# Score tiles of four heads with 32 queries each instead of two heads with 64, in an attention kernel on one core

## The reference

```python
# x: (4, 1024, 512); 16 query heads, 8 key heads, 128 plain and 64 rotated places a head
xn = layernorm(x)
c_Q = rms_norm(xn @ Wq_down, q_norm_w)                 # 192 wide
q_nop, q_pe = c_Q @ Wq_up, c_Q @ Wq_pe                 # 16 heads x 128, 16 heads x 64
c_KV = rms_norm(xn @ Wkv_down, kv_norm_w)              # 128 wide
k_nop, v = split(c_KV @ Wkv_up)                        # 8 heads x 128 each, used by two query heads
k_pe = rms_norm(xn @ Wk_pe, k_pe_norm_w)               # 64, shared by all heads
q = concat(q_nop, rope(q_pe)); k = concat(k_nop, rope(k_pe))
scores = (q . k) / sqrt(192), masked to k <= q
y = softmax(scores) @ v
out = x + y @ Wo + ternary(xn) @ (ternary(weight) + rram).T
```

## Time and profile before

| | |
|---|---|
| median of 3 runs | 1685.34 us (1685.02 to 1686.73) |
| the profiled execution | 1687.18 us, its span 1685.4 us |
| PE busy | 1647.7 us, 98% of the span |
| DVE busy | 1309.9 us, 78% |
| ACT busy | 1117.6 us, 66% |
| GpSimd busy | 599.7 us, 36% |
| matmuls | 11656 |

### The profile page before, as it was taken

The page is one execution under the profiler, slowest core; times in us unless marked ns, Lnnn a source line. Parts: engine busy times, 40 slices in busy tenths (PEclk is TensorE's granted clock), DMA queues, the critical chain, the costliest instruction groups (busy, mean ns, idle before and its releaser), DMA issues.

```text
span 1685.4 us, 34179 instructions
## 1 busy us (share of the span) xinstructions
PE 1647.7 (98%) x11656; PEld 929.4 (55%) x11656; DVE 1309.9 (78%) x3369; ACT 1117.6 (66%) x2464; POOL 599.7 (36%) x1080
## 2 busy tenths in 40 slices
PE   5989999999999999999999999999999999999999
PEld 5755555555555556555554555555555555655544
DVE  5888878768788788778878787876878878877765
ACT  5877767567676676657667676766767667666663
POOL 2433334333343333433433333433334333343330
PEclk9999999999999999999999999999999999999999
DMA  9346777758768677786759867775876867776776
GB/s 261 88 74 114 128 133 126 131 109 144 136 126 148 115 132 133 147 135 105 141 102 156 144 127 133 129 128 109 147 133 131 147 112 134 136 138 132 132 134 123
DMA packets 780264, 221.25 MB, mean 131 GB/s; under 512 B 766968, under 2 KB 769402, under 8 KB 779770
## 3 DMA queue, kind: packets, MB, share of 16 engines
q1 hardware_dynamic: 769392, 195.41, 66.9%
q10 hardware_dynamic: 9162, 17.37, 3.5%
q0 software_dynamic: 1536, 6.29, 1.1%
HBM read 19.76 MB, written 8.39 MB: 17 GB/s over the span
## 4 chain that ended last, share of the span: by engine, by line
PE 86%; DVE 4%; issue 3%; ACT 2%; POOL 2%; DMA 2%; SPq 0%; DVEq 0%; ACTq 0%; POOLq 0%
PE bank L729 7%; PE bank L731 7%; PE bank L730 7%; PE bank L732 7%; PE bank L827 6%; PE bank L829 6%; PE bank L828 6%; PE bank L774 5%; PE bank L776 5%; PE bank L775 5%; PE bank L742 4%; PE bank L484 2%; PE bank L485 2%; PE bank L785 1%; PE bank L523 1%
## 5 line engine op out<-in xcount | busy, mean ns | idle before, releaser
L1116 ACT ACTIVATE P<-P,nm 128x256 f32<-128x256 f32 (+15 forms) x512 | 381.8, 746 | 409.9 <-DVE nm L1520 409.1
L1520 DVE CUSTOM_DVE_ANT_0 P<-bank,mask,neg 128x256 f32<-128x256 f32 (+15 forms) x512 | 383.1, 783 | 244.6 <-PE bank L742 237.8
L1769 POOL TENSOR_SCALAR sn<-sm 128x1 f32<-128x1 f32 x512 | 207.8, 406 | 888.3 <-ACT P L1116 877.4
L1111 ACT ACTIVATE F<-P,rc 128x256 f16<-128x256 f32 (+15 forms) x512 | 365.2, 741 | 102.3 <-DVE rc L1528 64.1
L1534 DVE SCALAR_TENSOR_TENSOR F<-P,rc,F 128x256 f16<-128x256 f32 (+15 forms) x512 | 402.4, 798 | 2.8 <-ACT F L1111 2.4
L729 PE MATMUL bank<-K,Q 128*128 128x512 f16 (+7 forms) x760 | 241.7, 319 | 0.0
L732 PE MATMUL bank<-K,QP 128*128 128x512 f16 (+7 forms) x760 | 241.7, 319 | 0.0
L730 PE MATMUL bank<-K,Q 128*128 128x512 f16 (+7 forms) x760 | 241.7, 319 | 0.0
L731 PE MATMUL bank<-K,Q 128*128 128x512 f16 (+7 forms) x760 | 241.7, 319 | 0.0
L827 PE MATMUL bank<-WO,YH 128*128 128x512 f16 x512 | 194.3, 379 | 5.0 <-DVE YL L1540 4.7
L828 PE MATMUL bank<-WO,YH 128*128 128x512 f16 x512 | 194.0, 379 | 0.0
(11 more groups left out here) (228 smaller groups left out, 3248.9 us busy)
## 6 DMA issues: line engine op xcount, KB each, us to landing
out<-X ACTq DMA_DIRECT2D x31, 256.0 KB, 2.8
X<-in_x ACTq DMA_DIRECT2D x28, 256.0 KB, 4.1
FT<-F SPq DMA_TRANSPOSE x348, 4.2
wo<-in_Wo POOLq DMA_DIRECT2D x4, 1024.0 KB, 7.1
V<-CC SPq DMA_DIRECT2D x64, 32.0 KB, 2.9
QP<-QS SPq DMA_TRANSPOSE x128, 2.7
X<-in_x SPq DMA_DIRECT2D x4, 256.0 KB, 8.4
kv<-in_Wkv_up POOLq DMA_DIRECT2D x1, 1024.0 KB, 12.3
```

The lines of the kernel that those rows point to most:

```text
L1111: return e.eng.activation(dst, src, ACT.Copy, scale=scale)
L1116: e.eng.activation(m.P[:, u % 4, 0:w], m.P[:, u % 4, 0:w], ACT.Exp, bias=m.nm[:, u % 8:u % 8 + 1], scale=-1.0, accum_out=m.sm[:, u % 8:u % ...
L1520: e.eng.tensor_tensor_reduce(out=m.P[:, u % 4, 0:w], in0=m.pS[u % 2][:, off:off + w], in1=m.mask[:, end - w:end], scale=m.neg[:, :], scala ...
```

## The change

Score tiles now hold four heads with 32 queries each. The rows of x are loaded in plain order. `row_block(u)` is 0, 2, 1, 3 for u%4 = 0, 1, 2, 3, and `columns` takes 96, 64, 32 or 0 keys off for row block 0, 1, 2, 3, in all units.

- `queries_hi`, `queries_lo`, `values_hi` and `values_lo` sort between "by heads" and "by rows" in pieces of 32; the stride of two that `values_hi` and `values_lo` wrote with is gone.
- SP turns `QS` into a new tile `QT`, and DVE copies that in the new order to `QP` (`rotated_rows`, L1351 of the changed kernel). In body n it does so for unit n+3, ahead of the two maxima of half 1. PE waits for that copy (`s.qp`), no longer for the DMA.
- `rotated_hi` and `rotated_lo` are two instructions each, on 64 partitions each.
- Columns between a tile's cut and the end of what is weighed have to be zero: GpSimd's `zero_gap(u)` (a MEMSET into `F`) follows `scale_sum(u)`. It waits until the slot of `F` has been turned (`ft_in`). In ordinary units there is one for u%4 = 0 and 1, in whole ones for 0, 1 and 2; 268 in all.
- GpSimd waits for its own results in a few places (`sm`, `gap`, `pl`).
- `keep_keys` and `KT` are gone: SP turns the keys into `K` directly. The values go to `V` in one DMA instead of two.
- `weigh_pair` waits for all four tiles of the last unit.

```diff
 def columns(u):
-    return blocks_wide(u) - (64 if side(u) == 0 and not whole(u // 4) else 0)
+    return blocks_wide(u) - 96 + 32 * row_block(u)
...
     def pair(n, p):
-        e.wait_ge(s.q_in[n % 2], 16 * (n // 2 + 1))
-        e.wait_ge(s.k_at, n // NG + 1)
+        e.wait_ge(s.qp, n + 1)
+        e.wait_ge(s.k_in, 16 * (n // NG + 1))
...
     def weigh_pair(p):
-        for z in (GROUP_OF[4 * n + p], GROUP_OF[4 * n + p + 2]):
+        for z in range(GROUP_OF[4 * n], GROUP_OF[4 * n + 3] + 1):
             e.wait_ge(s.ft_in[z % FSLOTS], 16 * (z // FSLOTS + 1))
...
     def rotated_hi(self, n):
-        e.eng.activation(rotated_parts(m, n)[0], m.R1.rearrange("p (g h) d -> p g h d", g=2), ACT.Copy).then_inc(s.ph, 1)
+        for a in range(2):
+            op = e.eng.activation(rotated_parts(m, n, a)[0], m.R1[64 * a:64 * a + 64, :, :], ACT.Copy)
+        op.then_inc(s.ph, 1)
...
+    def rotated_rows(self, n):
+        e, m, s = self.e, self.m, self.s
+        e.wait_ge(s.q_in[n % 2], 16 * (n // 2 + 1))
+        if n >= 2:
+            e.wait_ge(s.s, 4 * (n - 1))
+        e.eng.tensor_copy(m.QP[:, n % 2, :, :].rearrange("p r (h k) -> p r h k", k=32),
+                          m.QT[:, n % 2, :, :].rearrange("p h (r k) -> p r h k", k=32)).then_inc(s.qp, 1)
...
+    def zero_gap(u):
+        slot, z, at = parts_place(u)
+        w, lo, end = columns(u), blocks_wide(u), gap_end(u)
+        if end == w:
+            return
+        if z >= FSLOTS:
+            e.wait_ge(s.ft_in[slot], 16 * (z // FSLOTS))
+        both = m.F[:, slot, at:at + 2 * lo].rearrange("p (x c) -> p x c", x=2)
+        e.eng.memset(both[:, :, w:end], 0.0).then_inc(s.gap, 1)
...
     outputs_lo(15)
+    queries.rotated_rows(2)
     for n in range(N):
...
+            if p and n + AHEAD + 1 < N:
+                queries.rotated_rows(n + AHEAD + 1)
             if u < 4 * N:
                 maximum(u)
```

## The result

The changed kernel takes **1699.25 us** (median of 4, 1697.59 to 1699.96) against 1685.5 for the kernel before in the same runs: ratio 1.0076, 95% interval 1.0064 to 1.0088. It is 13.8 us slower by the medians (10.8 to 14.8 by the interval), where 1687.4 was forecast, and lies outside the range, 1678 to 1694. The profiled execution took 1699.09 us with a span of 1697.1.

The account below looks back on a forecast made before the run. TensorE, busy 98% of the span, was taken as the bound, so time is columns plus its waits. Columns −13.9, start +3.9, repeats +9.6 and end +2.5 sum to +2.1 on 1685.34: 1687.4 us, range 1678 to 1694.

Parts of the forecast that it names:

- Columns, −13.9: TensorE's score passes over the whole kernel: fewer columns from the new cuts save 13.9 us.
- the 29 that was charged: Some 60 passes of 32 columns on TensorE: charged 29 ns each instead of 16, taking 0.8 us off the saving.
- The end, +2.5: First `weigh_pair` of the last unit: it now waits for the last tile, costing 2.5 us net.
- the clock decides nothing: Whole kernel: the granted clock stands at its full 2.4 GHz in every slice, so it was given no cost.
- The second `rotated_hi`: ScalarE's chain to `queries_hi`: the added instruction delays it by 0.31 us, between 0 and 0.40.
- The copy: VectorE ahead of half 1's maxima: 0.35 us, free where VectorE idles, counted in full where it is busy.
- The start, +3.9: From `pair(2, 0)` through the first bodies: the late copy and longer chains add 3.9 us of waiting and lost saving.
- The repeats, +9.6: Three repeats where a long tile precedes short ones: longer chains add 3.2 us of waits each, 9.6 in all.
- The 0.06 us that was read as cover near 836: Second part of a repeat: TensorE starts 0.06 us after `values_lo` ends, taken as all the slack there.
- That waits don't add up: Rival for the repeats: one longer wait shrinks the next, so they cost 2.6 us in all; 1680.4 us, chance 0.33.
- The meeting with GpSimd: Rival: the copy runs beside GpSimd's work and takes 0.33 us more in 19 places; 1693 us, chance 0.20.
- GpSimd's stall on the gap: Rival: `zero_gap` waits and holds up `scale_sum`, 0.1 us in each of 116 units' bodies; 1695 us or more, chance 0.05.

Follow-up runs that it names:

- e8_both: Changed kernel without VectorE's copy (TensorE reads QT directly) and with one `rotated_hi` and one `rotated_lo`, some score parts on wrong rows: 1671.80 us.
- b12_end: Kernel before the change, with only `weigh_pair` made to wait for all four tiles of the last unit: 1689.05 us.
- b11_hi2: Kernel before the change, with only `rotated_hi` split into two instructions of 64 partitions: 1712.57 us.
- e3_one: Changed kernel with `rotated_hi` and `rotated_lo` as one 128-partition instruction each, half the rows having high and low parts swapped: 1675.39 us.
- e14_apart: Changed kernel with the first `rotated_hi` left ahead of `queries_hi` and the second moved behind `values_hi`: 1692.58 us.
- e2_late: Changed kernel with the copy of half 1 moved from ahead of the two maxima to behind them: 1693.51 us.
- e13_behind: Changed kernel with both `rotated_hi` behind `queries_hi`, and behind `values_hi` too where that stands next: 1694.91 us.
- e15_behind_late: e13_behind with the copy moved behind the two maxima: 1691.53 us.
- e4_nogap: Changed kernel without the MEMSETs of the gaps from unit 20 on, so stale numbers are weighed there: 1699.44 us.

## Why the prediction was wrong

- **Columns, −13.9: right.** Undisturbed bodies are 0.09 to 0.10 us shorter, and a pass of 32 columns starts 0.03 us before the next, no more than one of 64. The mean over the passes is 26 ns against 29, so the 29 that was charged was near, and the 16 by the formula alone is not what the trace shows:

```profile
775.12 0.18 PE L729 MATMUL bank<-K,Q 128*128 128x32 f16 x1
775.15 0.18 PE L730 MATMUL bank<-K,Q 128*128 128x32 f16 x1
```

  With the copy and both second instructions out (e8_both), the loop is 15.7 us shorter than before, MEMSETs and all: 2 more than its columns, as it waits a little less.
- **The end, +2.5: right**, 2.5 us of waiting at L810 and b12_end. The profiled execution lost 1.5 more there at half the clock, which nobody had priced: the prediction took the page's slices to say that the clock decides nothing.
- **The second `rotated_hi`: this is the step that failed.** It was put at 0.31 us and counted only where TensorE already waited for `queries_lo`, 3 times outside the start. It is 0.54 us, and it opened waits for `queries_lo` in 15 places where none stood, and small delays in 42 bodies (b11_hi2); alone it costs 24.3 to 26.0 us, where all work added outside the end was put at 13.5. VectorE waited for `queries_hi` 60 times before and TensorE felt it in 7 places; the others were taken to have ample slack, and b11_hi2 shows that in 15 more there was less than what one instruction adds. The delay also isn't over when TensorE has been served: `queries_lo` stands ahead of `values_lo`, the next maxima and `scaled_lo` in VectorE's list, and in bodies of short tiles these have no idle time in between. In body 42 of the changed kernel VectorE comes to the first maximum of half 1 8.10 us after the body's start, in e3_one 7.57, before the second instruction of that body is even run. How the rest of its cost comes about is open, as e14_apart shows.
- **The copy: its length was right, its wait was missed.** 0.35 us was taken, 338 ns is the mean and 0.29 the usual value. The prediction never looked when the DMA of QT lands. Before, QP had until TensorE's next pair; now VectorE needs it half a body earlier, and where SyncE has x, keys and values to move first it isn't there, in 29 of 128 cases, all in the fourth unit of a tile (bodies 3, 7, 11 and on). SyncE's timeline ahead of the one in body 43:

```profile
597.92 1.44 SPq L1839 DMA_TRANSPOSE XT<-XS  x1
599.53 1.45 SPq L1859 DMA_TRANSPOSE C<-CC  x1
601.03 1.26 SPq L1861 DMA_TRANSPOSE K<-CC  x1
602.33 0.60 SPq L1863 DMA_DIRECT2D V<-CC  x1
603.10 3.07 SPq L1923 DMA_TRANSPOSE FT<-F  x1
606.29 1.20 SPq L1905 DMA_TRANSPOSE QT<-QS  x1
```

  The maxima stand behind the copy. In the changed kernel's timeline of VectorE:

```profile
608.76 0.29 DVE L1351 COPY QP<-QT 128x512 f16<-128x512 f16 x1 [2.65 <-DMA QT<-QS]
609.10 0.68 DVE L1536 CUSTOM_DVE_ANT_0 P<-bank,mask,neg 128x448 f32<-128x448 f32 x1
```

  The maximum starts at once; before, in the same body, it waited 3.22 us for TensorE. The 2.65 us mostly replace that idle time: moving the copy (e2_late) gave 5.7 us in all, not 61.
- **The start, +3.9: too small.** The copies for units 0 and 1 hold the first score by 1.65 us, and the one for unit 2 `pair(2, 0)` by 1.87:

```profile
77.76 0.19 PE L708 MATMUL bank<-K,Q 128*128 128x32 f16 x1 [1.65 <-DVE QP L1351]
...
97.60 0.19 PE L729 MATMUL bank<-K,Q 128*128 128x32 f16 x1 [1.87 <-DVE QP L1351]
```

  `pair(2, 0)` starts at 97.60, not 96.4, since VectorE's list itself was later: it comes to this copy at 97.26, where it was done with the last product for Wo by 95.99 before. The same short section led to 96.60, 97.00 and 96.88 in e2_late, e13_behind and e15_behind_late, none of which has a stretch at half the clock ahead of body 0, so 96.4 was nearer than the one profile says. By body 22 the loss is 5.15, with 3.7 us of columns saved: 8.9 against 3.9. This too is mostly the second instructions: bodies 0 to 21 take 240.28 us in e3_one and 245.32 in the changed kernel.
- **The repeats, +9.6:** they lost 1.5, 1.1 and 2.2 us net of 0.093 × 32 = 3.0 of columns each, so 4.5, 4.1 and 5.2 of waits, 13.8 in all. Forecast and profiled execution lie 9.8 us apart; the start is 5.0 of them, the repeats 4.2 and the clock at the end 1.5, less about 1 of small differences the other way. The 0.06 us that was read as cover near 836 is none: in all 56 marked waits of TensorE at L827 and L552 before, L829 and L543 in the changed kernel and L827 in b11_hi2, the start comes 0.056 us or more after VectorE's end, 0.057 as a rule. TensorE was waiting there already, without a mark: that matmul starts 0.37 us after the one ahead of it (835.47, 512 columns), where 0.22 is usual.
- **The rivals.** That waits don't add up was wrong in sign: they came to more than one by one. The meeting with GpSimd was not it: beside GpSimd the copy does take 0.75 us (below), but only 20 of the 128 copies took over 0.4, and 7 of these stand in bodies 117 to 123, which lost nothing. GpSimd's stall on the gap exists and costs nothing (e4_nogap).

The direction was thus argued from the right kind of mechanism, a chain without cover. Its price was drawn from the waits that the trace marks, and these only show where the cover had long run out.

## What to carry to other kernels

An instruction added to a chain of several engines costs where the slack is smaller than it, not only where a wait stands already: measure the slack at every use (the release against the use, in each body) before pricing it, and if in doubt add the instruction to the kernel before, alone; here one instruction of 0.4 us on an engine busy for 66% cost 26 us. When a buffer's reader changes from TensorE to an engine in the middle of the chain, look up when the buffer is filled as well as how long the copy takes. Splitting an instruction by partitions made neither half shorter here. A forecast for a long kernel should also look at the granted clock by short stretches, since a page of 40 slices doesn't show 3.4 us at half of it.

## What the runs showed of the hardware

- ScalarE's copy of 64 x 256 takes 406 to 407 ns and that of 128 x 256 400 ns; two in a row (partitions 0 to 63, then 64 to 127) hold the next one back by 0.85 us, a single one by 0.31. Behind one on partitions 0 to 63 the next on 128 partitions started after 0.31 us too (e14_apart, 114 bodies); behind one on 64 to 127 nothing started before 0.44.
- VectorE copies 128 x 512 from f16 to f16 in 0.28 us, and from partitions 0 to 63 to 64 to 127 (64 x 256) in 0.22 to 0.24. Beside an operation of GpSimd that began first it took 0.75, and ended 0.15 after it, in the changed kernel:

```profile
99.82 0.75 DVE L1351 COPY QP<-QT 128x512 f16<-128x512 f16 x1
...
99.70 0.72 POOL L1717 TENSOR_TENSOR R<-R,R 128x256 f32<-128x256 f32 x1
```

- A wait costs TensorE more than its mark: where L543 waited 6.9 us in 11 places, the distances from start to start were 8.8 us longer than the columns ask, 0.17 us more at each, and at L829 7.6 us for 5.6 in 12 places, 0.16 more at each. It is what a matmul otherwise overlaps with the next one: 0.38 us of duration against 0.22 from start to start.
- TensorE's granted clock fell to 0.50, 1.2 GHz, for 3.4 us at a time (once 6.8) in 16 of the 19 profiled executions, each time ahead of body 4 or in the last 20 us. From 1681.89 to 1684.87 in the changed kernel 14 matmuls of 256 columns took 2.98 us, where 0.109 from start to start, as at full clock, makes 1.53.
